# A decoder in seven stages on one core: row moments made by the stage that finishes a sequence, shared expert first, output by pairs

## The reference, cut to what matters

```python
x = x + attention(ln(x))            # 16 heads of 16, weights w_qkv, w_out            "attention 0"
x = x + cross(ln(x), ctx)           # softmax over projections of ctx, applied to ln(x) "cross 0"
x = x + ffn(ln(x))                  # weights round-tripped through NF4, hidden 704     "feed-forward"
x = x + mamba(ln(x))                # 8 heads, chunks of 32, causal convolution         "Mamba"
x = x + cross(ln(x), ctx, pos)      # 32 heads of 8, rotary by position                 "cross 1"
x = x + block(ln(x))                # r = ln(x); r = r + attention(rms(r) * ln1)        "attention 1"
                                    # return r + moe(rms(r) * ln2)                      "experts"
```

```python
def ln(x):  return (x - mean(x)) / sqrt(var(x) + 1e-5)      # over the 256 numbers of a row
def rms(r): return r / sqrt(mean(r * r) + 1e-5)
def moe(t): # t is 1024 x 256
    s = sigmoid(t @ Wr);  idx = top_k(s + bias, 8);  w = s[idx] / sum(s[idx])
    routed = sum over the 32 experts e of w[e] * ((silu(t @ Wg[e]) * (t @ Wu[e])) @ Wd[e])
    return routed + (silu(t @ Wsg) * (t @ Wsu)) @ Wsd       # the shared expert
```

## Time and profile before

| what | us |
|---|---|
| median of 3 runs | 1581.68 (1578.65 to 1584.42) |
| profiled execution | 1579.09, its span 1577.0 |
| load stage | 0 to 7.4 |
| attention 0 | 7.4 to 154.9, PE busy 114.7 |
| cross 0 | 156.2 to 197.3, PE busy 24.8 |
| feed-forward | 198.0 to 315.9, PE busy 88.7 |
| Mamba | 316.8 to 525.7, PE busy 184.0 |
| cross 1 | 526.6 to 736.0, PE busy 162.5 |
| attention 1 | 737.0 to 1254.7, PE busy 475.2 |
| experts | 1255.7 to 1570.9, PE busy 290.1 |
| store stage | 1571.8 to 1577.0 |

### The profile page before, as it was taken

The page is one execution under the profiler, slowest core; times in us unless marked ns, Lnnn a source line. Parts: engine busy times, 40 slices in busy tenths (PEclk is TensorE's granted clock), DMA queues, the critical chain, the costliest instruction groups (busy, mean ns, idle before and its releaser), DMA issues. The chain is left out here.

```text
span 1577.0 us, 23655 instructions
## 1 busy us (share of the span) xinstructions
PE 1340.0 (85%) x8475; PEld 982.5 (62%) x8509; DVE 957.4 (61%) x1620; ACT 793.3 (50%) x1594; POOL 612.4 (39%) x523
## 2 busy tenths in 40 slices
PE   4787648989799379995779999999999769999997
PEld 3564435744377244442657777777777558888886
DVE  4762466468744578773567777777877454343443
ACT  2464111435442136664376877877878334444441
POOL 4210010001053431102556666666765335555552
PEclk8999759989999678897799999999999969999998
DMA  2000040030000100002000000000000123233321
GB/s 69 1 2 4 14 103 1 1 102 0 1 1 1 37 1 2 2 2 79 7 8 21 15 21 21 15 21 21 15 21 8 27 79 117 98 112 116 114 97 49
DMA packets 29551, 56.11 MB, mean 36 GB/s; under 512 B 6429, under 2 KB 16093, under 8 KB 29264
## 3 DMA queue, kind: packets, MB, share of 16 engines
q1 hardware_dynamic: 29456, 54.85, 10.8%
HBM read 53.52 MB, written 1.22 MB: 35 GB/s over the span
## 5 line engine op out<-in xcount | busy, mean ns | idle before, releaser
L2576 DVE TENSOR_TENSOR e_act<-e_gated,ps 128x512 f32<-128x512 f32 x66 | 45.4, 688 | 165.2 <-POOL e_gated L2426 165.2
L1840 POOL TENSOR_TENSOR a_raw<-a_prod 128x512 f32<-128x512 f32 x72 | 99.3, 1379 | 51.0 <-DVE a_prod L2262 51.0
L1845 POOL TENSOR_TENSOR a_q_low<-a_raw,a_q_high 128x512 fp32r<-128x512 f32 x64 | 82.9, 1295 | 87.4 <-ACT a_q_high L2116 87.4
L2426 POOL TENSOR_TENSOR e_gated<-e_gate,e_wb 128x512 f32<-128x512 f32 x66 | 85.2, 1293 | 56.2 <-ACT e_gate L2509 44.7
L2259 DVE TENSOR_TENSOR a_prod<-ps,a_rot 128x512 f32<-128x512 f32 x72 | 49.7, 691 | 94.0 <-PE ps L1901 93.8
L2124 ACT ACTIVATE a_shift<-ident,a_nmax 128x128 bf16<-128x128 f32 x256 | 82.0, 392 | 32.2 <-DVE a_nmax L2271 31.6
L1849 POOL TENSOR_TENSOR a_o_low<-a_o,a_o_high 128x512 fp32r<-128x512 f32 x64 | 82.6, 1290 | 37.6 <-ACT a_o_high L2167 35.6
L2417 POOL TENSOR_TENSOR e_we_low<-e_we,e_we_high 128x768 fp32r<-128x768 f32 x33 | 60.8, 1843 | 90.7 <-ACT e_we_high L2514 90.7
L1611 DVE SCALAR_TENSOR_TENSOR m_acc<-ps,m_conv_w,m_acc 128x1020 f32<-128x1020 f32 (+2 forms) x60 | 76.1, 1275 | 28.1 <-ACT m_acc L1506 26.7
L2509 ACT ACTIVATE e_gate<-ps 128x512 f32<-128x512 f32 x66 | 39.5, 598 | 105.2 <-PE ps L2466 105.2
L575 DVE TENSOR_REDUCE x_nmax<-ps 128x2 bf16<-128x512 f32 x128 | 82.6, 690 | 11.6 <-PE ps L349 11.2
(11 more groups left out here) (451 smaller groups left out, 4171.5 us busy)
## 6 DMA issues: line engine op xcount, KB each, us to landing
e_wb<-token_weights SPq DMA_DIRECT2D x33, 512.0 KB, 4.0
e_we<-in_experts SPq DMA_DIRECT2D x33, 384.0 KB, 3.1
a_wq<-in_a_wq SPq DMA_DIRECT2D x16, 256.0 KB, 2.7
a_wo<-in_a_wo SPq DMA_DIRECT2D x16, 256.0 KB, 2.6
m_win<-in_m_winT SPq DMA_DIRECT2D x2, 1024.0 KB, 8.9
nf_pickU<-in_nf_pickU SPq DMA_DIRECT2D x2, 768.0 KB
nf_raw<-in_ffn_w SPq DMA_DIRECT2D x3, 352.0 KB
x<-in_x SPq DMA_DIRECT2D x1, 1024.0 KB
```

The costliest lines, as they stand in the source:

```text
L1840: e.tensor_tensor(raw[:, i % 2, :], prod[:, i % 2, 0, :], prod[:, i % 2, 1, :], ALU.add).then_inc(s_raw, 1)
L1845: e.tensor_tensor(low_part, raw[:, i % 2, :], high_part.bitcast(F32), ALU.subtract).then_inc(s_xl, 1)
L2426: e.tensor_tensor(gated[:, half, :], gate[:, half, :], wb[:, s % SLOTS, half * BANK:(half + 1) * BANK], ALU.mult).then_inc(s_gw, 1)
```

## The change

Each `step` increments a semaphore and waits for it. In all six stages before the experts, GpSimd's four calls stand behind all else in its list, and VectorE's stand behind each `add`:

```diff
                 ... core.x[:, 2 * b:2 * b + 2, :] ... ALU.add).then_inc(s_add, 1)
-            moments(0)
-            moments(1)
-            normalise(0)
-            moments(2)
-            moments(3)
-            for b in range(1, B):
+                e.wait_ge(s_add, b + 1)
+                ahead.vector(e, b)
+
+            if not rope:
+                moments(0)
+                moments(1)
+                normalise(0)
+                moments(2)
+                moments(3)
+            for b in range(0 if rope else 1, B):
                 normalise(b)
```

The load stage is gone; attention 0 loads x by pairs (and is the one stage that still makes its own moments), and its constants and memsets come first on GpSimd. In cross 1 too the memsets come first:

```diff
@@ small_head_attention, sync @@
+            if not rope:
+                e.dma_start(core.x[:, 0:2, :], x[:, 0:2, :]).then_inc(s_x[0], 16)
+                e.dma_start(core.ident[:], io["ident"]).then_inc(s_ident, 16)
             e.dma_start(wq[:], ...).then_inc(s_wq, 16)
...
             e.dma_start(wk[:], ...).then_inc(s_wk, 16)
+            if not rope:
+                for b in range(1, B):
+                    e.dma_start(core.x[:, 2 * b:2 * b + 2, :], x[:, 2 * b:2 * b + 2, :]).then_inc(s_x[b], 16)
@@ gpsimd @@
-            e.tensor_copy(ident16[:], core.ident[:]).then_inc(s_id, 1)
-            for b in range(B):
-                (variance, power of pair b; behind the first one the four memsets)
+            if not rope:
+                e.memset(core.minus_half[:], -0.5).then_inc(s_set, 1)
+                e.memset(core.ones_row[:], 1.0)
+            (the four memsets)
+            if not rope:
+                (variance, power of pair b; behind the first one ident16 and bq)
+            else:
+                e.tensor_copy(ident16[:], core.ident[:]).then_inc(s_id, 1)
@@ scalar @@
-            if rope:
-                e.wait_ge(s_rt, 5)
-                e.activation(trig[:], turns[:], ACT.Sin).then_inc(s_rt, 1)
             for at in range(FIRST, LAST):
                 slot, p = at // 2, at % 2
+                if rope and at == FIRST + 1:
+                    e.wait_ge(s_rt, 5)
+                    e.activation(trig[:], turns[:], ACT.Sin).then_inc(s_rt, 1)
```

In cross 0 the scalings and the transposes stand ahead of the projections and their bias additions instead of behind them. In the feed-forward, Mamba and attention 1 the statistics, aggregates and powers at the start are deleted. Attention 1 makes `normed` for all pairs first and `res` last:

```diff
@@ stage_attention_1, vector @@
-            moments(0)
-            moments(1)
             normalise(0)
-            moments(2)
             normalise(1)
-            moments(3)
+            normalise(2)
+            normalise(3)
             e.wait_ge(s_ln1, 16)
-            h_low(0)
-            normalise(2)
-            h_low(1)
-            normalise(3)
-            h_low(2)
+            for b in range(3):
+                h_low(b)
             e.wait_ge(s_rot, 16)
             rotate(0)
             h_low(3)
             for i in range(1, FIRST):
                 rotate(i)
+            for b in range(B):
+                residual_of(b)
+            e.wait_ge(s_res, NT)
```

In the expert stage the shared expert becomes number 0 and the routed ones 1 to 32, so that the first expert doesn't need the router; its row of weights is a memset of `wb[:, 0, :]` and `wT` has 32 rows. Each pair is scaled, transposed, copied with ln2, made high (now by ACT, it was VectorE) and low by itself. TensorE's order:

```diff
-            rn.tensor(e)
-            (router product)
-            (turn the router's weights)
-            e.wait_ge(s_wt, 3)
-            e.wait_ge(s_tl, 1)
-            up(0, 0)
+            (transposes by pair)
+            def route_between():
+                route()                               # the router product
+                e.wait_ge(s_tl, NT // 2)
+
+            e.wait_ge(s_tl, NT // 4)                  # low parts of the first two pairs
+            up(0, 0, route_between)                   # called between its two halves
+            turn_weights()
             with e.Fori(0, NE // SLOTS) as i:
                 for s in range(SLOTS):
                     up(i, s + 1)
                     down(i, s, s == 0, s == SLOTS - 1)
-            down(NE // SLOTS - 1, SLOTS, True, True)
+            e.wait_ge(s_xa, NE // SLOTS * 4 + 1)
+            for t in range(NT):
+                if t % 4 == 0:
+                    e.wait_ge(s_al, 2 * NE + t // 4 + 1)
+                (three products of tile t)
+                if t % 2:
+                    mm.then_inc(s_pair, 1)
```

On ACT the high part of expert 0's weights stands ahead of the pairs' copies and waits for that expert's transfer, which SP now issues first. On GpSimd the low part of expert 0 and then x + res (line 2411 before) stand behind all scalings. At the end VectorE adds each pair as soon as its six products are done, and SP sends it:

```diff
-            add(NE // SLOTS, 1)
+            for tp in range(NT // 2):
+                e.wait_ge(s_pair, tp + 1)
+                e.tensor_tensor(core.x[:, 2 * tp:2 * tp + 2, :], core.x[:, 2 * tp:2 * tp + 2, :],
+                                ps[:, 4 + tp, :]..., ALU.add).then_inc(s_sum, 1)
@@ sync @@
+            for pair in range(NT // 2):
+                e.wait_ge(s_sum, pair + 1)
+                e.dma_start(out[:, 2 * pair:2 * pair + 2, :], core.x[:, 2 * pair:2 * pair + 2, :]).then_inc(s_out, 16)
+            e.wait_ge(s_out, 16 * (NT // 2))
@@ stages @@
-STAGES = [load_stage, stage_attention_0, stage_cross_0, stage_ffn_0, stage_mamba_1, stage_cross_1,
-          stage_attention_1, stage_moe_1, store_stage]
+STAGES = [stage_attention_0, stage_cross_0, stage_ffn_0, stage_mamba_1, stage_cross_1,
+          stage_attention_1, stage_moe_1]
```

## The result

| | before | changed |
|---|---|---|
| median | 1580.16 us (4 runs, 1578.27 to 1584.42) | 1559.26 us (4 runs, 1558.09 to 1560.00) |
| ratio | | 0.9865, 95% interval 0.9849 to 0.9882 |
| profiled execution | 1579.09, span 1577.0 | 1558.09, span 1556.3 |

The forecast was 1560, with a range of 1552 to 1571. The time is 20.9 us shorter, and the sum said 21.75. (The kernel before was measured at 1581.68 when the forecast was made and at 1580.16 here.) That the total agrees so well is partly luck: taken stage by stage, terms miss by up to 5.1 us one way (attention 0) and 3.9 the other (cross 1). The table cuts both profiled executions at the same events, the end of each stage's last addition to x (or res); a tail and its barrier thus count with the stage that follows.

A forecast was written before the change was run, and what follows sets the result against it. TensorE, busy 85%, bounds the stages; gains lie in its waits at the eight borders. Heads and end -41.75, tails +14.7, groups +5.3 sum to -21.75: time 1557.3, 1560 against the median, range 1552 to 1571.

The forecast's parts named there:

- The tails: Statistics, aggregates and GpSimd's steps between a stage's last addition and the barrier: +14.7 us over six stages.
- The groups inside loops: Three groups of statistics per stage, 1.05 us of VectorE each, delay TensorE where VectorE is full: +5.3, bounds 0 and 9.5.
- the rival "slower": Each of nine groups in loaded loops opens a gap that lowers TensorE's clock; over 3.5 us a group, 0.3% slower; chance 0.03.
- Attention 0's head: Load stage and barrier go, x arrives by pairs, statistics from about 7.5 to 9: -4.9, bounds -3 and -6.5.
- Cross 0: Scalings and transposes run while weights load, so scores come at 10.2 or less after the begin: -11.8; with groups and tail -8.05.
- Feed-forward and Mamba: Feed-forward: a small operation's clash with GpSimd moves, -2.0, net +0.15. Mamba: first product's transfer wait, -0.5, net +2.35.
- Cross 1: Memsets delay the first scaled pair to +5.3; first rotation at +11.0 instead of +17.5: -6.5, net -1.15.
- the rival "larger gain": VectorE gets in between GpSimd's instructions: 3 us more in cross 1, res scalings' 1.5 falls away; -26, 1556; chance 0.10.
- Attention 1: Low parts of h come earlier, -4.2; eight moved res scalings ahead of the loop cost 1.5: net -2.7.
- Expert stage: Shared expert runs beside the router's chain, saving its 8.85 us; first down at 1293.5 for 1299.7: -6.1 including 2.75 of tail.
- The end: Each pair is added and sent while TensorE makes the next: -4.5, bounds -4 and -5.
- the rival "smaller gain": Heads give less as VectorE starves beside GpSimd: 13.2 less together, 1573; most of them, about 1569; chance 0.27.

The follow-up runs named there:

- the reordered version: Changed kernel with attention 0's first pair scaled ahead of the second pair's moments: 1557.18 us, ratio 0.9848.
- the repeat: The changed kernel measured once more, nothing edited: 1560.20 us, ratio 0.9861.
- the version with nothing beside the router's chain: Changed kernel with the router's product and the turning of the weights ahead of both halves of the shared expert: ratio 0.9897.
- groups deferred: Changed kernel with all four sequences' statistics made behind the last addition in five stages: 1571.93 us, ratio 0.9955.
- `ln2` alone: Changed kernel with ACT's copies in the expert stage waiting for ln2 only, not also w_r and the bias: 1564.02 us, ratio 0.9891.
- router first: Changed kernel with the router's product before both halves of the shared expert instead of between them: 1559.29 us, ratio 0.9860.
- identity copy first: Changed kernel with GpSimd's identity copy ahead of its four memsets in cross 1: 1562.43 us, ratio 0.9889.
- cross 0 in its old order: Changed kernel with cross 0's projections and bias additions again ahead of scalings and transposes, moments still made ahead: 1563.88 us, ratio 0.9907.
- the version with all edits: Changed kernel with edits to attention 0, cross 1, the expert stage and the last product together: 1565.87 us for 1599.46, ratio 0.9786.

## Why the prediction was right, point by point

- **What bounds the kernel, and the forecast's direction.** Right: the gain lies at the borders, and no loop got faster but by the clock (cross 1's and the last stage's last product).
- **The tails.** Right and the best of the terms: from last addition to next begin 2.12, 2.11, 2.11 and 2.12 more, 3.41 after cross 1 and 2.68 after attention 1; 14.55, forecast 14.7.
- **The groups inside loops.** The sum, 5.3, was fair, the places were wrong. Cross 1, charged 2.0, lost 0.3 between its first and last row maximum. Attention 0, charged 1.0, lost 4.1: the group at 101.8 cost 2.5, with a fall of the clock right behind it, and the last product ran slow for 1.6; moving that group alone took both away, but the 1.6 also comes and goes without it (see there). This is the mechanism that I had as the rival "slower", at one place; the rival needed it at all nine. Cross 0, charged 1.6, lost 1.4 between its first row maximum and its last addition.
- **Attention 0's head.** -2.9 for -4.9. The step "statistics from about 7.5 to 9" failed: the second pair's data came at 10.0. That this arrival holds the head was right, as the reordered version shows. I had also misread the row for it: 4.7 is the landing of b_v, a transfer of 128 KB and the stage's fourth, not the seventh; the same view has 5.1 for the 256 KB of w_v and w_o, and x's second pair took 5.8 (4.16 to 10.0).
- **Cross 0.** -12.3 at the scores for -11.8, groups 1.4 for 1.6. The first row maximum came another 0.9 earlier, since the first score product ran at full clock (1.99 for 3.75).
- **Feed-forward and Mamba.** The small operation's clash went (-1.6 by then, -2.0 charged), and Mamba's head won the time of its transfer. But in the feed-forward a slow stretch at 240.6 and other clock phases took 2.1 back in products that nobody had edited, and in Mamba 1.7, ahead of its first group.
- **Cross 1.** The right number, +11.15 for +11.0, by a wrong step. I wrote that "some 5 us of memsets from the barrier on put the first pair at +5.3"; it was scaled at +2.2, since VectorE got in once between every two memsets, as the rival "larger gain" had it. The copy of the identity behind the memsets held TensorE to +5.4 in its place. I had looked at VectorE's neighbours on GpSimd, not at what TensorE waits for. By the rule of the Trainium skill ("SBUF — State Buffer", "Who interferes with whom") that a lock is held for one instruction, this trace agrees, with 1.05 beside 0.95, 1.11 beside 1.10 and 3.10 beside 2.88. The trace of the kernel before agrees only in part, as I had written: of the 4.93 us of its two scalings the first took 1.91, across two memsets of 0.95, and the second 3.10 beside the one of 2.88. The stage's last product, at full clock, took 1.97 instead of 3.65, which is most of the rest.
- **Attention 1.** The low parts' gain came, 4.6 at the first row maximum for the 4.2 forecast, and the 1.5 for the eight moved scalings did not: at the 17th row maximum, 93 us into the stage, 5.5 were won. In the repeat it was 4.5 there.
- **Expert stage.** -3.6 from last addition to first down for -6.1. The step "what is saved is the shared expert's 8.85 us that ran after the router" was too large: the overlap is worth 4.9, as the version with nothing beside the router's chain has it. Two things were late: ACT, behind the bias's transfer, of which I had only the bound -4, and the low parts behind x + res, which I did not have at all. Together with the router's place they were worth 5.7. The end gave -4.5 from the end of TensorE's last product on, as forecast, and the last product itself 1.5, at full clock where before it had met a slow stretch from 1564.5 on: chance covers part of the miss.
- **Sums and signs.** The terms of the rival "smaller gain" add up to 12.9, not 13.2. Of the signs of being wrong that I had named, two came: cross 1's first scalings ended before the memsets did, and TensorE stood idle for ACT in the expert stage's first half (4.72 us at 1255.48). A third came at one place, 2.5 us for one group in attention 0. Of the signs of being right, cross 1's loop did not get 2 us longer (0.3), and the first down came 41.4 after the last addition, not 39. So the forecast held as a sum, and the mechanism failed in cross 1, in attention 0's groups and in the expert stage's overlap.

What stays open: no run put back the load stage, attention 1's old order of scalings or the old end, so their terms are read from the two profiles alone. Also open is why cross 1 took 3.0 more with its groups deferred, and what sets whether a stage's last product runs slow; no run separates these from the clock's phase.

## What to carry to other kernels

When work is moved across a border, list for each engine the first instruction that another engine waits for, and what stands ahead of it in its own list: here an identity copy behind memsets, a second pair's arrival ahead of the first pair's scaling, and GpSimd's x + res and a bias behind a shared semaphore ahead of the low parts and the copies. The first held a head for 2.3 us, the second for 3.6, and the last together with the router's place for 5.7. A group of one microsecond in a full loop can cost two and a half when it lowers TensorE's clock, so it goes where the engine has idle time. Judge edits of a few microseconds by the stretch between barriers, not by the whole time.

## What the runs showed that I had not expected

**A race for one instruction decides 1.1 us, some 20 times.** In attention 1's loop 29 of the 32 instructions of VectorE's L2289 start beside one of GpSimd's L1861, nearly all within 0.05 us. In one case VectorE's takes 0.48 and GpSimd's 1.58; TensorE waits for neither. In the other GpSimd's takes 1.27 and VectorE's 1.60, and TensorE, which waits 0.55 for it, has its further products 1.12 us later. The first pair of rows is of the changed kernel (timeline), the second of the version with nothing beside the router, at the same point of the loop.

```profile
868.75 0.48 DVE L2289 SCALAR_TENSOR_TENSOR a_inv_split<-a_inv_high,a_odd,a_inv 128x256 fp32r<-128x256 f32 x1
...
868.79 1.58 POOL L1861 TENSOR_TENSOR a_raw<-a_prod 128x512 f32<-128x512 f32 x1 [0.52 <-DVE a_prod L2266]
```

```profile
872.45 1.60 DVE L2289 SCALAR_TENSOR_TENSOR a_inv_split<-a_inv_high,a_odd,a_inv 128x256 fp32r<-128x256 f32 x1
...
872.50 1.27 POOL L1861 TENSOR_TENSOR a_raw<-a_prod 128x512 f32<-128x512 f32 x1 [0.52 <-DVE a_prod L2266]
```

Of the 32 such instructions 7 were long in the changed kernel and in the one before, 8 in the repeat, 10 in the two whose attention 1 took some 4 us more (`ln2` alone, router first), and on the third chip 20, 21, 26 and 28. There attention 1 took 532.0, 534.4, 539.0 and 541.1, for 516.5 with 7: 21 more long ones by 1.12 make 23.5 of 24.5 us. The order of the recorded starts tells half of it. In six or seven of the 29 pairs GpSimd's start comes first or within 0.01 of VectorE's, and there VectorE's was long in every one of the 14 profiles; in the other 22 or 23 VectorE's start is some 0.05 ahead, as in both pairs of rows above, and there it was short 22 times in the changed kernel and once in the version with nothing beside the router. What tips those I can't tell, and no run changes them by an edit. The spread of one line shows how it went (ns least/median/most):

```profile
L2289 DVE SCALAR_TENSOR_TENSOR a_inv_split<-a_inv_high,a_odd,a_inv x32: 484/1601/1602, 795.2 to 1253.8; 128x256 fp32r<-128x256 f32 x32
```

**The same code meets the slow stretches of the clock at other points.** The same code of attention 0 took 155.6 to 156.5 in eight executions and 152.28 in one. Its first slow stretch began at 24.2 there, and between 21.8 and 23.2 in the eight. Nor do the falls always recur where all before them recurs. The repeat and the version with the router first have the same falls within 0.1 us up to 333.2, in Mamba. Then the lower clock lasts 6.8 us in the one and 3.4 in the other, and the next fall comes at 401.4 and at 425.3 (windows of each; columns as in the earlier trace rows).

```profile
400.00:405.00 5.00, 3.73 (x8) 2.10 (x9) 4.93 (x6) 1.52 (x2) 0.00 (x0) 0.66 0.00 0
```

```profile
400.00:405.00 5.00, 4.66 (x14) 2.05 (x14) 3.85 (x5) 1.53 (x2) 0.00 (x0) 1.00 0.00 0
```

Four executions went the second way (ln2 alone, router first, identity copy first, cross 0 in its old order). Their first addition in Mamba comes 1.0 us earlier than in the changed kernel, but 1.6 us are lost between the first and the second, where a fall of the clock lies (at 483.3 with the router first), and the stage is no shorter: 213.6 to 213.7, for 213.0 to 213.3. So a gain of 2.3 at a head can be 0.5 near the end, as in cross 1 with the identity copy first, or 3.3, as in the version with all edits.
